# Causal mask and row maximum in one VectorE instruction, in place of mask matmuls on TensorE

## What is computed

```python
score = jnp.einsum('bhqd,bhkd->bhqk', q, k) / math.sqrt(HEAD_DIM)
causal = jnp.tril(jnp.ones((S, S), dtype=bool))
score = jnp.where(causal[None, None], score, -jnp.inf)
attn = jax.nn.softmax(score, axis=-1)
out = jnp.einsum('bhqk,bhkd->bhqd', attn, v)
...
x = x + _L0_attn_ref(_layernorm(x, axis=-1), ...)
```

## Time and profile before

| | before |
|---|---|
| median of three runs | 1020.1 us |
| the profiled execution's own time | 1017.27 us |
| its span, first to last instruction | 1015.5 us |
| TensorE busy | 748.8 us |
| VectorE busy | 574.9 us |
| ScalarE busy | 400.9 us |
| GpSimd busy | 257.4 us |
| mean granted TensorE clock | 0.826 of full speed |

### The profile page before, as it was taken

The page is one execution under the profiler, slowest core; times in us unless marked ns, Lnnn a source line. Parts: engine busy times, 40 slices in busy tenths (PEclk is TensorE's granted clock), DMA queues, the critical chain, the costliest instruction groups (busy, mean ns, idle before and its releaser), DMA issues.

```text
span 1015.5 us, 14363 instructions
## 1 busy us (share of the span) xinstructions
PE 748.8 (74%) x4837; PEld 373.1 (37%) x4855; DVE 574.9 (57%) x1526; ACT 400.9 (39%) x612; POOL 257.4 (25%) x477
## 2 busy tenths in 40 slices
PE   3579999989878710899999336878888895724775
PEld 1344545443434610466666221212222223512332
DVE  6676777763443650244444148797899833355554
ACT  1226565655454100122222022467677682211433
POOL 5544455663220147000000373241100001010000
PEclk9778999996778555799999755799999996555998
DMA  6635644462130001111111143021221000000001
GB/s 182 207 125 156 179 136 152 149 173 69 51 93 14 1 28 52 32 34 34 37 34 32 34 143 125 22 68 61 104 64 43 23 1 0 1 0 0 1 1 41
DMA packets 80792, 68.61 MB, mean 68 GB/s; under 512 B 15826, under 2 KB 75474, under 8 KB 80722
## 3 DMA queue, kind: packets, MB, share of 16 engines
q1 hardware_dynamic: 72482, 60.10, 19.0%
q0 software_dynamic: 2048, 4.20, 1.4%
q10 hardware_dynamic: 6192, 3.41, 1.1%
HBM read 37.24 MB, written 29.99 MB: 66 GB/s over the span
## 4 chain that ended last, share of the span: by engine, by line
PE 55%; DVE 19%; issue 8%; POOL 6%; ACT 6%; DMA 3%; SPq 1%; another core or an unknown queue 1%; DVEq 0%; POOLq 0%
DVE mx L526 10%; PE bank_pv L649 9%; PE bank_turn L510 8%; PE bank_st L1516 4%; PE bank_turn L1516 4%; PE bank_turn L1820 4%; PE bank_st L1532 4%; PE bank_st L614 3%; POOL routed_tokens L1457 3%; PE bank_turn L668 2%; PE bank_st L1525 2%; DVE xn L372 2%; PE bank_turn L710 2%; PE bank_turn L448 1%; DMA stk<-stack_kx 1%
## 5 line engine op out<-in xcount | busy, mean ns | idle before, releaser
L526 DVE TENSOR_REDUCE mx<-bank_turn 128x1 f32<-128x512 f32 (+3 forms) x512 | 296.6, 624 | 73.4 <-PE bank_turn L510 38.3
L629 ACT ACTIVATE probs<-bank_st 128x1024 f32<-128x1024 f32 (+4 forms) x288 | 243.3, 882 | 156.3 <-PE bank_st L614 153.8
L510 PE MATMUL bank_turn<-stk 64*128 64x512 bf16 (+4 forms) x768 | 184.2, 320 | 45.3 <-DVE mx L526 32.0
L614 PE MATMUL bank_st<-stk 64*128 64x512 bf16 (+4 forms) x576 | 177.1, 372 | 2.4 <-ACT probs L629 1.7
L649 PE MATMUL bank_pv<-probs,vsl 128*32 128x512 f32 (+4 forms) x1152 | 143.5, 572 | 4.4 <-POOL probs L637 4.1
L510 PEld LDWEIGHTS bank_turn<-stk 64*128 64x128 bf16 x768 | 60.2, 101 | 179.3 <-DVE mx L526 101.5
L1467 POOL DMA_INDIRECT w<-expert_outputs,place_u x32 | 31.5, 983 | 174.4 <-DMA expert_outputs<-probs 165.3
L448 PE MATMUL bank_turn<-ident,xn 128*128 128x128 f32 x80 | 20.2, 401 | 74.5 <-DVE xn L372 73.4
L637 POOL TENSOR_SCALAR_AFFINE_SELECT probs<-probs 128x256 f32<-128x256 f32 x128 | 51.8, 407 | 69.1 <-ACT probs L629 67.5
L538 POOL CAST neg<-mx 128x16 bf16<-128x16 f32 x48 | 9.6, 200 | 228.5 <-DVE mx L526 225.3
L404 POOL TENSOR_TENSOR rstd<-var,mhalf 128x4 f32<-128x4 f32 x24 | 25.3, 1055 | 129.5 <-DVE var L363 129.5
(11 more groups left out here) (249 smaller groups left out, 1132.2 us busy)
## 6 DMA issues: line engine op xcount, KB each, us to landing
stk<-stack_A SPq DMA_DIRECT2D x64, 256.0 KB, 3.1
w<-in_M_w SPq DMA_DIRECT2D x12, 512.0 KB, 4.4
stack_A<-parts SPq DMA_DIRECT2D x15, 384.0 KB, 2.7
stack_A<-fill SPq DMA_DIRECT2D x8, 512.0 KB, 4.7
stk<-stack_X SPq DMA_DIRECT2D x16, 256.0 KB, 2.7
stack_A<-parts SPq DMA_DIRECT2D x15, 256.0 KB, 3.1
routed_tokens<-zero SPq DMA_DIRECT2D x1, 2560.0 KB, 11.1
probs<-routed_tokens SPq DMA_DIRECT2D x40, 64.0 KB, 1.7
```

The costliest lines, as they stand in the source:

```text
L510: mm = e.matmul(o, stk[r, slot, 0, pp, qt * P:(qt + 1) * P], stk[r, slot, 1, pp, 0:keys], start=True, stop=not a.causal)
L526: e.tensor_reduce(o.rearrange("p h q -> p q h"), bank_of((g, m))[:, 0:k * keys].rearrange("p (q h k) -> p q h k", q=len(tiles), h=len(hs)) ...
L614: mm = e.matmul(bank_st[j][0:a.kp, pp, 0:S - q0], stk[r, slot, 1, pp, kt * P:kt * P + a.kp], stk[r, slot, 0, pp, q0:S], start=True, stop=True)
L629: e.activation(probs[0:a.kp, probs_of(g, kt), j:HG:2, 0:n], bank_st[j][0:a.kp, :, 0:n], ACT.Exp, scale=1 / math.sqrt(HD)).then_inc(s["prob ...
```

## The change

Each item of A0 becomes one query tile and one head, so that a unit has 16 items in place of 12, in the order of rising width: four of 128 keys, four of 256, four of 384, four of 512. The two mask matmuls behind each score matmul are left out. VectorE takes an item with `tensor_tensor_reduce`: it adds a constant bf16 tile `ahead_of` (0, or -1e30 ahead of the diagonal) to the scores, multiplies by -1, writes the product back over the scores in PSUM, and keeps the minimum as the item's negative maximum. The slice `ahead_of[:, S - keys:S]` has its diagonal block at the end for every width. GpSimd makes one constant of 512 columns in place of four of 256. A1 and X0 keep `tensor_reduce`.

```diff
--- before.py
+++ after.py
@@ -73,10 +73,7 @@
         if keys < P:
             self.items = [item(q, 2, j, 2, keys) for j in (1, 0) for q in range(0, QT, 2)]
         elif causal:
-            self.items = [item(0, 1, 1, 2, P), item(1, 1, 1, 2, 2 * P), item(0, 1, 0, 2, P),
-                          item(2, 1, 1, 1, 3 * P), item(2, 1, 0, 1, 3 * P), item(1, 1, 0, 2, 2 * P),
-                          item(2, 1, 3, 1, 3 * P), item(3, 1, 1, 1, 4 * P), item(2, 1, 2, 1, 3 * P),
-                          item(3, 1, 3, 1, 4 * P), item(3, 1, 0, 1, 4 * P), item(3, 1, 2, 1, 4 * P)]
+            self.items = [item(q, 1, h, 1, (q + 1) * P) for q in range(QT) for h in (1, 3, 0, 2)]
         else:
             self.items = [item(q, 1, h, 1, keys) for q in range(QT) for h in (1, 3, 0, 2)]
 
@@ -208,9 +205,7 @@
         identb = sb("identb", [P, P], BF16)
         ones_row = sb("ones_row", [1, P])
 
-
-        pair_q, even_q = sb("pair_q", [P, 2 * P], BF16), sb("even_q", [P, 2 * P], BF16)
-        behind_pair, behind_even = sb("behind_pair", [P, 2 * P], BF16), sb("behind_even", [P, 2 * P], BF16)
+        ahead_of = sb("ahead_of", [P, S], BF16)
         parts = sb("parts", [P, 2, 3, S], BF16)
         rest = sb("rest", [P, 2, S])
         vraw = sb("vraw", [P, NT, D])
@@ -490,9 +485,6 @@
         def rows_of(j):
             return slice(HR * j, HR * (j + 1))
 
-        def half(t, j):
-            return t[rows_of(j), P * j:P * (j + 1)]
-
         def max_pe(e, g, m):
 
             a, slot = layer(g), g % UNITS
@@ -508,11 +500,7 @@
                     o = bank[:, at:at + keys]
                     at += keys
                     mm = e.matmul(o, stk[r, slot, 0, pp, qt * P:(qt + 1) * P], stk[r, slot, 1, pp, 0:keys],
-                                  start=True, stop=not a.causal)
-                    if a.causal:
-                        o = o[:, qt * P:(qt + 1) * P]
-                        e.matmul(o, half(pair_q, j), half(behind_pair, j), start=False, stop=False)
-                        mm = e.matmul(o, half(even_q, j), half(behind_even, j), start=False, stop=True)
+                                  start=True, stop=True)
             mm.then_inc(is_filled((g, m)), 1)
 
         def max_dve(e, g, m):
@@ -523,6 +511,10 @@
                 wait(e, s["neg"], g - 1)
             e.wait_ge(*filled((g, m)))
             o = mx[:, g % 2, hs.start % 2, hs.start // 2:hs.start // 2 + len(hs), tiles.start:tiles.stop]
+            if a.causal:
+                e.tensor_tensor_reduce(bank_of((g, m))[:, 0:keys], bank_of((g, m))[:, 0:keys], ahead_of[:, S - keys:S], -1.0, 3e38,
+                                       ALU.add, ALU.min, o.rearrange("p h q -> p (h q)")).then_inc(is_emptied((g, m)), 1)
+                return
             e.tensor_reduce(o.rearrange("p h q -> p q h"),
                             bank_of((g, m))[:, 0:k * keys].rearrange("p (q h k) -> p q h k", q=len(tiles), h=len(hs)),
                             AX.X, ALU.max, negate=True).then_inc(is_emptied((g, m)), 1)
@@ -1955,7 +1947,7 @@
 
         @block.tensor
         def _(e):
-            e.wait_ge(s_const, 5)
+            e.wait_ge(s_const, 4)
             first_stream_pe(e)
             moe_pe(e, 2)
             second_stream_pe(e)
@@ -2007,20 +1999,10 @@
 
             e.affine_select(out=before[:], in_=onesb[:], compare_op=ALU.is_gt, fill=0.0, base=0,
                             pattern=[[1, P]], channel_multiplier=-1)
-            for t in (pair_q, even_q):
-                e.memset(t[:], 1.0)
-            for t in (behind_pair, behind_even):
-                i = e.memset(t[:], MASKED)
-            i.then_inc(s_const, 1)
+            e.memset(ahead_of[:], 0.0).then_inc(s_const, 1)
             e.wait_ge(s_const, 2)
-            for t, op, base in ((pair_q, ALU.is_ge, 0), (even_q, ALU.is_equal, 0), (behind_pair, ALU.is_ge, -2),
-                                (behind_even, ALU.is_equal, -1)):
-                i = e.affine_select(out=t[:], in_=t[:], compare_op=op, fill=0.0, base=base,
-                                    pattern=[[1, 2 * P]], channel_multiplier=-2)
-            i.then_inc(s_const, 1)
-            e.wait_ge(s_const, 3)
-            e.affine_select(out=pair_q[:], in_=pair_q[:], compare_op=ALU.is_ge, fill=0.0, base=1,
-                            pattern=[[-1, 2 * P]], channel_multiplier=2).then_inc(s_const, 1)
+            e.affine_select(out=ahead_of[:], in_=ahead_of[:], compare_op=ALU.is_ge, fill=MASKED, base=S - P,
+                            pattern=[[-1, S]], channel_multiplier=1).then_inc(s_const, 1)
             e.tensor_copy(identb[:], ident[:]).then_inc(s_const, 1)
             first_stream_pool(e)
             moe_pool(e, 2)
```

## The result

The changed kernel takes 1035.95 us, the median of four runs (1033.71 to 1039.83), against 1018.55 for the kernel before (1012.91 to 1020.37). The ratio is 1.0184, with a 95% interval of 1.013 to 1.0239: it is slower by 1.8%. The forecast was 1019 us and no change. Runs of one kernel lie up to 15 us apart (the kernel before, in all groups of runs, from 1008.9 to 1024.3), so differences of a few us between single profiled executions say little.

What follows compares the result with a forecast made beforehand. TensorE was taken to bound the first layer's loop, its gain just eaten by VectorE: 1017.3 - 1.8 (set-up) + 3.1 (first units) + 0.7 (loop) = 1019.3, forecast 1019 us, no change; range 1004 to 1045, the forecast's own 1010 to 1027.

Steps and rivals of the forecast that it cites:

- -19.9 for the masks: First layer's loop: removing the two mask matmul lines saves 19.9 us if nothing else binds.
- The set-up: GpSimd's shorter constant set-up before the loop: VectorE's first statistic starts 1.8 us earlier, near 6.0.
- -1.8 + 3.1 = +1.3: Ahead of the loop: set-up 1.8 us earlier, against maxima of the first two units longer by 0.8 and 2.3.
- the half rate: Rival: the new VectorE instruction runs at two cycles a column, near 1100 us; chance 0.03.
- F = 0.19: Fixed us per VectorE item in the loop: 0.097 as a reduce plus 0.09 read-out, giving 38.3 us a batch.
- A dear instruction: Rival: the new VectorE instruction's fixed part is 0.26 to 0.35 us, giving 1037 to 1060 us; chance 0.33.
- The prediction's own sign: Loop batch under 39 or over 44 us means the fixed part per VectorE item is outside the range taken.
- a mis-sized ring: Sign for the loop: if the fixed part is right but the batch is not, the ring of banks is mis-sized.
- 2.95: Us a batch that VectorE loses to waits in the unit with merge and projection, taken from the third layer.
- the faster rival: TensorE's floor of 35.3 us a batch nearly reached in the loop: 1004 us, down to 997; chance 0.20.
- the later finish costs nothing while the ring runs ahead: In the first layer, a unit's later finish adds no time while the ring of banks runs ahead.
- The clock rival: Waits for VectorE cause TensorE clock dips of a microsecond or two; ten give +15, 1035 us; chance 0.04.

Runs made afterwards that it cites:

- e1: The kernel before with only its two mask matmuls left out, same 12 items and reduce: 1000.9 us, ratio 0.9855 to before.
- e6: The changed kernel with one item of each width per chunk, tensor_reduce in place of the new instruction and no mask: 1018.8 us, ratio 1.0029 to before.
- e7: The changed kernel in its own rising order, with tensor_reduce in place of the new instruction and no mask: 1027.6 us, ratio 1.0087 to before.
- e2: The kernel before with the changed kernel's 16 single items in rising order, mask matmuls and reduce kept: 1032.5 us, ratio 1.0162 to before.
- e8: The e5_packed kernel with the new instruction's product written to a bf16 tile in SBUF instead of PSUM: 1007.8 us, ratio 0.989 to before.
- e10: The e1 kernel with A0's items using only two of the three banks, unless both are on loan: 1016.6 us, ratio 1.0032 to before.
- e3: The changed kernel with its 16 items reordered so that each chunk gets one of each width: 1019.5 us, ratio 1.0025 to before.
- e5_packed: The changed kernel with the 12-item list of before, the new instruction called once a head: 1006.8 us, ratio 0.9868 to before.

## Why the prediction was wrong

**Where it went.** By ratios the way from before to after is: masks off -1.45% (e1), items split in even order +1.74% (e6), rising order +0.58% (e7), new instruction in that order +0.97% (after). The sum is +1.84%. In us that is -15, +18, +6 and +10. The last two steps are barely clear of noise, the second is not in doubt. The prediction had -19.9 for the masks, and put the rest on the instruction alone.

**What was right.** The set-up: the first statistic starts at 6.07, where the prediction said near 6.0.

```profile
6.07 0.29 DVE L352 BATCH_NORM_STATS2 stats<-x_sb 128x6 f32<-128x128 f32 x1
```

The time up to the first mark grew by 0.9 us, where the sum had -1.8 + 3.1 = +1.3. The column rate is 1.04 ns, so the half rate is out. The layers behind stayed as they were. The read-out's row of 0.14 us lay between the bounds.

**F = 0.19 was wrong, and it was not the main cause.** The spacing was to be 0.72 and measured 0.65, so F is 0.115 for the pair. The term that was mis-sized is the read-out, taken as 0.09 from ScalarE's pair. The pair costs 0.02 to 0.05 more than a reduce alone (0.097 from the third layer; in e2 four reduces of 512 columns stand in 2.49 us, which leaves 0.07), so the read-out costs at most that. VectorE's need is 5.33 + 16 x 0.115 + 0.66 = 7.8 us a unit, and 33.5 a batch in place of 38.3. A dear instruction, my largest rival, is excluded: it gave 1037 us, close to the measured 1036, but with F = 0.26, and that is an accident. The prediction's own sign read a batch over 44 us as an F outside what I took. F is outside, but on the cheap side, where the sum gives a shorter batch; so what is left of the sign is its last part, a mis-sized ring. The Trainium skill, page "Vector Engine (DVE) Microarchitecture Reference", § 5.2 "Measured stream behaviour on trn2", has about 75 ns for this fixed part; the rows have 115 with its output in PSUM and, from e8, 0.61 - 0.533, near 80 with its output in SBUF.

**The steps that broke the sum.** With the measured F my own scheme gives 33.5 + 2.95 = 36.4 us a batch, and some 16 us gained in 3.5 batches. The batches took 47.3 on the mean (141.84 / 3), with VectorE busy 35.1 of them: 13.8 us above VectorE's need, where the sum had 2.95. So the loss is in two other steps of the prediction: the term for the waits between the engines, and the price of the clock.

*The item list was costed at nothing beyond its fixed parts.* The 2.95 us a batch for waits between the engines came from the third layer, where VectorE is the bound and every item is equal, and I carried it over to a list of unequal items. In the first layer neither engine is the bound on the mean; they take turns. While VectorE has 512-wide items, at 0.65 us each, TensorE waits for banks: of the 16.3 us that it stood idle ahead of items in the twelve units, 5.0 are ahead of the 512-wide ones and 6.3 ahead of the 128-wide ones that come next. With the narrow ones, at 0.25 us for 128 columns, VectorE catches up and waits, most of all ahead of the 384-wide (15.0 us, against 1.7 ahead of the 512-wide, in the groups above). How far one engine may be ahead is set by the three banks and what each holds. Narrow items alone in a bank leave most of it empty. The packed list holds 5120 / 12 = 427 columns a bank on the mean, the single items 320; three banks hold 1280 against 960, and e10's two packed ones 853. That these columns are the measure is argued and not shown. I had written that three banks let TensorE run ahead by about 2 us only, and that 70% of the columns fall into two chunks, but only against the faster rival, and never as a price. That "the later finish costs nothing while the ring runs ahead" assumed what it should have shown.

*The clock rival had 0.04.* It named the larger of two losses. The split of the 18 us is gaps +11.7, clock +14.9 and work -8.6. Its time, 1035, was nearly right, but by ten dips of 1.5 us, where there were fewer and longer ones. Before has one dip in the twelve units, at 99 to 103 us (the one of the earlier trace rows). After has five:

```profile
99.00:112.00 13.00, 11.65 (x59) 3.49 (x59) 7.61 (x29) 4.41 (x9) 3.49 (x10) 0.52 0.37 108
133.00:140.00 7.00, 6.85 (x41) 2.57 (x39) 3.82 (x18) 3.95 (x5) 1.71 (x6) 0.55 0.25 81
147.00:154.00 7.00, 5.75 (x32) 1.71 (x33) 4.18 (x27) 3.38 (x5) 4.51 (x9) 0.53 0.31 87
195.00:199.00 4.00, 4.00 (x22) 1.29 (x22) 1.90 (x10) 1.81 (x3) 3.89 (x7) 0.57 0.45 127
224.00:231.00 7.00, 6.17 (x41) 2.73 (x41) 3.94 (x19) 3.84 (x6) 2.97 (x8) 0.64 0.18 44
```

Smaller windows around the first show how one goes:

```profile
96.00:100.00 4.00, 2.00 (x17) 0.71 (x18) 1.77 (x10) 2.83 (x4) 2.69 (x10) 0.95 0.71 252
100.00:104.00 4.00, 4.00 (x19) 0.78 (x19) 1.81 (x9) 1.51 (x2) 0.81 (x2) 0.50 0.36 122
104.00:108.00 4.00, 3.97 (x23) 1.39 (x23) 2.73 (x10) 1.19 (x2) 0.81 (x2) 0.50 0.57 159
108.00:112.00 4.00, 3.68 (x21) 1.32 (x17) 3.06 (x10) 0.77 (x2) 1.46 (x5) 0.50 0.24 60
```

TensorE was busy 2.00 of 4 us from 96 to 100, then ran at 0.50, which is its level of 1.2 GHz, for 12 us. Before, it was busy 2.44 of the same 4 us, and the clock of the next 4 was 0.68 and of those behind 1.00:

```profile
96.00:100.00 4.00, 2.44 (x29) 1.36 (x25) 1.81 (x5) 3.13 (x5) 1.33 (x5) 0.89 0.50 180
100.00:104.00 4.00, 4.00 (x30) 1.46 (x33) 2.03 (x5) 1.16 (x2) 0.68 (x2) 0.68 0.79 208
104.00:108.00 4.00, 4.00 (x55) 2.29 (x47) 3.40 (x7) 1.82 (x5) 2.27 (x7) 1.00 0.51 170
```

I had priced a dip at "a microsecond or two". A stretch of 12 us at half the clock costs up to 6. This hole is not a wait for VectorE: it is the bank with `cos_sin`, 1.89 us after and 1.56 before. The same hole stands in every run, and what followed it differs. In e1 (1.57 us) and e2 (1.84 us) the clock did not fall at all. Here is e2, 97 to 105 us:

```profile
97.00:101.00 4.00, 1.99 (x26) 0.90 (x24) 1.10 (x5) 2.83 (x4) 2.52 (x9) 1.00 0.65 207
101.00:105.00 4.00, 3.80 (x43) 1.98 (x40) 2.94 (x9) 1.86 (x3) 0.82 (x2) 1.00 0.39 130
```

So a hole can bring a dip and need not. The other four dips of the changed kernel have only shorter single waits ahead of them, the longest of 1.29 us for VectorE, at 192 us. Their number and length differ from list to list, each seen in one execution. My evidence against, that the third layer kept 1.00 behind VectorE, was of a stretch in which equal items give one steady pace, and it did not carry over. The Trainium skill, page "TensorE: Matmul & The Clock Gate", § "A second HAM failure mode: psum-queue depth-cycling", describes a kernel whose TensorE idles briefly while it cycles through PSUM banks, and whose clock swings between the two levels. The rows agree in that the clock swings between 1.00 and 0.50.

**What stays open.** Splitting the items and taking a bank away have the same price in the time (e6 and e10 against e1), and both lengthen the waits for banks. This supports the ring, but the gaps grew to 21.2 us in e6 and only to 11.3 in e10, so the two do not lose in the same way. And no run kept the 16 turns and gave them more room, so whether the number of turns or the columns held in a bank decides is not separated. Nor is the place of the finish, or which score matmuls have a partner on the other rows. The 3 to 6 us of work by which the split differs between kernels with the same matmuls may be such lost partners or the roughness of the split. Why even single items lose by gaps (e3, e6) and rising ones by the clock (after, e7), with gaps of about the same sum, is not shown. Neither is what decides whether a hole brings a dip, or how long it lasts.

## What to carry to other kernels

When an edit changes how work is cut into buffers, cost the cut by itself: how many columns the ring holds, and how long the slower engine of each stretch takes for them, before and after. A mean need below the bound says nothing where two engines take turns at being the slower one; and a hole that this makes in TensorE can be priced twice, once as a wait and once as a lower clock behind it. Here the instruction cost little, and keeping the old packed list (e5_packed, 1006.8 us) turns a loss of 1.8% into a gain of 1.3%.

## What the runs showed of the hardware

The accumulator's read-out on VectorE costs little in its queue: its row of 0.14 us (0.08 where the main output goes to SBUF) starts together with the next main instruction, and the pair costs 0.02 to 0.05 us more than a reduce. ScalarE's held its next one back by 0.09.

An instruction that reads and writes PSUM and reads an SBUF tile keeps one column in 1.04 ns: back to back it took 0.25 us at 128 columns and 0.65 at 512. The pair's fixed part is 0.115 us, near 0.08 with the output in SBUF. With equal columns a row is longer than its cost in the queue: 0.73 against 0.65 at 512.

Half the clock stayed for 12 us behind one hole of 2 us, although TensorE was busy 3.97 of 4 us in it, and in e10 for 20 us with TensorE busy 18.71 of them. Before, behind a hole of 1.6 us, it was back within 4 us, and in e2, behind one of 1.84 us, it did not fall.
